# An expert layer whose routing is done ahead of its input rows: logits as products of their own, low parts between the routing steps

## The reference

```python
ys = y * scale
d = rsqrt(einsum('bi,io->bo', ys * ys, weight * weight) + EPS)
y = einsum('bsi,io->bso', x * ys[:, None, :], weight) * d[:, None, :]

lang_probs = softmax(y @ lang_w.T + lang_b)                    # 4 languages
expert_weights = lp_pad[..., idx] + lp_pad[..., idx + 1]       # sums of neighbours
router_probs = softmax(y @ router_w.T + router_b + 0.1 * expert_weights)
top_p, top_i = top_k(router_probs, 2); top_p = top_p / top_p.sum(-1, keepdims=True)
h = gelu(einsum('bsd,edh->bseh', y, w1) + b1, approximate=False)   # 256 -> 1024
expert_out = einsum('bseh,ehd->bsed', h, w2) + b2                  # 1024 -> 256
return x + (top_p[..., None] * take_along_axis(expert_out, top_i)).sum(axis=2)
```

## Time and profile before

| | us |
|---|---|
| median of 3 runs (296.48 to 300.69) | 298.55 |
| the profiled execution | 297.96 |
| its span in the profile | 296.2 |
| TensorE busy | 272.3 |
| ScalarE busy | 195.7 |
| VectorE busy | 189.2 |
| GpSimd busy | 179.4 |
| HBM read and written | 27.61 MB and 9.64 MB |

### The profile page before, as it was taken

How to read it: one execution, slowest core, us unless ns; L and a number is a source line. 1 busy time by engine, 2 the same in 40 slices (tenths; PEclk the granted TensorE clock), 3 DMA queues, 4 the chain that set the end, 5 groups by cost and what they waited for, 6 DMA issues and landing times.

```text
span 296.2 us, 8964 instructions
## 1 busy us (share of the span) xinstructions
PE 272.3 (92%) x3066; PEld 223.1 (75%) x3066; DVE 189.2 (64%) x427; ACT 195.7 (66%) x426; POOL 179.4 (61%) x161
## 2 busy tenths in 40 slices
PE   8999988689999999999999999999999999999800
PEld 6878967588889998777777777777787878778400
DVE  1857788799699788565565565555655656556410
ACT  3356469599697898757767677677676676775500
POOL 8200056884666598676878577777767776464230
PEclk9999999979999999999999999999999999999975
DMA  6899996399874333465574644853544434323130
GB/s 145 325 400 388 353 348 206 109 314 460 306 191 90 56 57 72 56 101 65 76 91 77 87 70 78 76 91 64 83 77 74 75 74 76 51 39 38 20 35 0
DMA packets 39497, 39.93 MB, mean 135 GB/s; under 512 B 19504, under 2 KB 35328, under 8 KB 39296
## 3 DMA queue, kind: packets, MB, share of 16 engines
q1 hardware_dynamic: 31872, 28.89, 32.8%
q0 software_dynamic: 7552, 10.45, 23.0%
q10 hardware_dynamic: 32, 0.01, 0.0%
HBM read 27.61 MB, written 9.64 MB: 126 GB/s over the span
## 4 chain that ended last, share of the span: by engine, by line
PE 82%; DMA 5%; DVE 4%; issue 3%; ACT 2%; POOL 1%; POOLq 0%; DVEq 0%
PE ps L643 33%; PE ps L660 30%; PE ps L539 5%; PE ps L652 4%; PE ps L557 4%; DMA rows<-y_rows,idx 3%; DMA out<-onehot,idx 3%; PE ps L481 1%; PE ps L620 1%; DVE wsp L951 1%; PE ps L512 1%; PE ps L521 1%; ACT wsp L781 1%; PE ps L497 1%; POOL out L470 1%
## 5 line engine op out<-in xcount | busy, mean ns | idle before, releaser
L643 PEld LDWEIGHTS ps<-onehot,wsp 128*128 (+1 forms) x1872 | 130.7, 99 | 34.4 <-issue 1.1
L643 PE MATMUL ps<-onehot,wsp 128*128 128x128 f16 x1872 | 154.2, 220 | 0.8 <-ACT onehot L811 0.6
L827 ACT ACTIVATE pay<-ps,cur 128x128 f32<-128x128 f32 x312 | 117.4, 459 | 51.7 <-issue 37.9
L660 PE MATMUL ps<-wsp,pay 128*128 (+1 forms) x616 | 138.1, 316 | 1.2 <-DVE pay L1113 1.2
L470 POOL DMA_INDIRECT out<-onehot,idx x39 | 67.8, 1739 | 33.7 <-DMA out<-onehot,idx 15.3
L1113 DVE SCALAR_TENSOR_TENSOR pay<-pay,cur 128x512 f16<-128x512 f32 x72 | 54.9, 762 | 29.2 <-ACT pay L815 27.9
L439 POOL DMA_INDIRECT rows<-y_rows,idx x39 | 57.0, 1463 | 17.9 <-issue 11.0
L461 POOL TENSOR_SCALAR onehot<-onehot,cur 128x256 f32<-128x256 f32 x36 | 38.1, 1059 | 24.0 <-DVE onehot L1131 15.8
L660 PEld LDWEIGHTS ps<-wsp,pay 128*128 128x128 f16 x616 | 45.7, 97 | 6.9 <-issue 1.7
L1107 DVE TENSOR_SCALAR pay<-pay,cur 128x512 f16<-128x512 f32 x36 | 18.8, 521 | 26.0 <-ACT pay L827 26.0
L815 ACT ACTIVATE pay<-pay,cur 128x512 f16<-128x512 f32 x36 | 26.0, 722 | 1.2
(11 more groups left out here) (176 smaller groups left out, 195.5 us busy)
## 6 DMA issues: line engine op xcount, KB each, us to landing
stage<-in_L_ffn_w SPq DMA_DIRECT2D x9, 1024.0 KB, 10.6
wsp<-in_L_ffn_w SPq DMA_DIRECT2D x7, 1024.0 KB, 12.0
y_rows<-pay SPq DMA_DIRECT2D x4, 512.0 KB, 9.3
wsp<-in_x SPq DMA_DIRECT2D x3, 512.0 KB, 7.9
b2bc<-in_L_ffn_b SPq DMA_DIRECT2D x1, 1024.0 KB, 4.8
rows<-y_rows,idx POOLq DMA_INDIRECT x39
out<-onehot,idx POOLq DMA_INDIRECT x39, 4.1
wsp<-in_x SPq DMA_DIRECT2D x2, 256.0 KB, 5.5
```

The costliest lines, as they stand in the source:

```text
L643: last = mm(ps[:, HB + (2 * j + g) % RING, c * P:(c + 1) * P], wsp[:, bass.ds(e, 1), o:o + P].rearrange("p a f -> p (a f)"), xsp[:, j % RI ...
L660: last = mm(ps[:, OB + j % 2, 0:width], hsp[:, (2 * j + g) % NH, part, c, :], wsp[:, bass.ds(e, 1), o + w:o + w + width].rearrange("p a f ...
L827: last = a.activation(to, ps[:, HB + (2 * j + g) % RING, c * P:(c + 1) * P], ACT.Gelu, bias=cur[:, j % CURS, cc:cc + 1], scale=cur[:, j % ...
```

## The change

1. **Logits first.** PE makes the logits of all 16 tiles by 32 products of 12 columns (`logits(t)`) between the last transposes, all into one bank; DVE adds the biases in one step of 192 columns. y's rows follow as products of 256 columns in three banks.
2. **Routing beside y's rows.** DVE's low parts of y, now `low_of_y`, stand two by two at eight places between routing steps (`ROWS_AT`). PE does rows 0 to 8 ahead of the counts, 9 to 12 behind them, then the first gram group and rows 13 to 15 among its sums. 19 `keep_warm` products are gone.
3. **Order of the rest.** The probabilities are stored by SP instead of POOL, ahead of y's third store. Gram groups 1, 2 and 3 stand behind the mapping products. POOL's scales of groups 1 and 2 stand among the gathers. ACT splits two halves in place of five ahead of tile 0; halves 4, 6 and 9 stand between copies and gelus.
4. **Experts by eights.** `BATCH` is 8: PE and DVE read `te` four times each (PE the first time ahead of tile 0, then where tiles 16, 24 and 32 begin).
5. **Tail.** ACT weighs tile 36 ahead of the last tile's first gelu instead of behind it.

```diff
-BANKS_Y = 5
+Y_BANKS = (0, 1, 3)
+ROWS_AT = {"in": (0, 1), "best": (2, 3), "second": (4, 5), "picked": (6, 7), "slots": (8, 9), "tiles": (10, 11), "half": (12, 13), "hot": (14, 15)}
-HIGHS = {0: (0, 2, 4, 6, 9), 1: (8, 3), 2: (7,), ...
+HIGHS = {0: (0, 2, 4, 6), 1: (9, 8, 3), 2: (7,), ...
-BATCH = 31
+BATCH = 8
...
             for c in range(4):
-                sp.wait_ge(y_split, 4 * c + 4)
+                sp.wait_ge(y_low, 4 * c + 4)
                 sp.dma_start(y_tiles[:, c // 2, c % 2 * 4:c % 2 * 4 + 4, 0:D],
                              payv[:, 4 * c:4 * c + 4, 0:D]).then_inc(y_written, 16)
...
                 if c == 1:
                     load_weights(9)
+                    sp.wait_ge(p_ready, 1)
+                    for b in range(NB):
+                        sp.dma_start(y_tiles[:, b, :, D:ROW], payv[:, b * TB:(b + 1) * TB, D:ROW]).then_inc(p_written, 16)
             load_weights(3)
             load_weights(7)
...
+            def logits(t):
+                pe.wait_ge(xt_ready, t // 2 + 1)
+                for k in range(KD):
+                    last = mm(ps[:, LB, t * NR:(t + 1) * NR], xT[:, t, k * P:(k + 1) * P], Wyr[:, t // TB, k, D:],
+                              start=(k == 0), stop=(k == KD - 1))
+                return last
             def rows_of_y(t):
-                pe.wait_ge(xt_ready, t // 2 + 1)
-                if t >= BANKS_Y:
-                    pe.wait_ge(lg_read, t - BANKS_Y + 1)
+                if t >= 3:
+                    pe.wait_ge(y_low, t - 2)
...
+            for t in range(9, 13):
+                rows_of_y(t)
+            pe.wait_ge(b1_max, 1)
+            mm(ps[:, SB, BS:BS + E], ...)
+            gram(0)
+            rows_of_y(13)
+            rows_of_y(14)
+            sum_squares(0)
+            rows_of_y(15)
             pe.wait_ge(tok_hot, 1)
...
             last.then_inc(mapped, 1)
+            gram(1)
+            pe.wait_ge(y_low, T)
+            gram(2)
+            sum_squares(1)
             gram(3)
-            keep_warm(WARM, 1, 512)
+            sum_squares(2)
...
             copy_x(0)
+            copy_sums(2)
             copy_x(1)
+            split_high(4)
             gelus(0, 0)
+            split_high(6)
             for j in range(NT):
-                if j == NT - 1:
-                    weigh(NT - 3)
                 gelus(j, 1)
...
+                if j == NT - 2:
+                    weigh(NT - 3)
                 if j + 1 < NT:
                     gelus(j + 1, 0)
...
+            def low_rows(name):
+                for t in ROWS_AT[name]:
+                    dve.wait_ge(y_high, t + 1)
+                    low_of_y(v, t).then_inc(y_low, 1)
...
             pick(0, route, 3, best)
+            scale_of_b1(0)
+            low_rows("best")
...
                 v.tensor_tensor(ohv[:, :, c0:c1], iota[:, :, c0:c1], ...).then_inc(hot_ready, 1)
+                if q == 1:
+                    low_rows("half")
+            low_rows("hot")
```

160 lines of the change are left out of this document (77 added, 83 removed).

## The result

The changed kernel takes **315.7 us**, median of four runs (313.0, 315.0, 316.4, 319.8), where the kernel before has 298.6 (296.5 to 300.7). The ratio is 1.055, interval 1.049 to 1.062. Medians here are of all runs of a kernel; ratios and their intervals leave out runs that were over 1.5% above its fastest. It is slower, as forecast, but by 17 us, not by 6.9, and lies above the range. The profiled execution is the fastest of the four, 313.04 us with a span of 311.3.

What follows compares the result with a forecast made beforehand. PE, busy 92% of the 296.2 us span and nearly unbroken after 60.0 us, passes any shift of the first expert blocks to the end. +6.2 + 1.8 + 0.3 - 1.4 = +6.9 on 297.96 gave 305 us, range 299 to 311.

Steps and rivals of the forecast that it cites:

- second 3 us behind, at 59: Weight halves 3 and 7, issued behind the last low part: first lands at about 56, second at 59; bounds 57 and 65.9.
- hidden behind this: Tile 0's gather lands at 57.8 us, before PE finishes waiting for halves 3 and 7, so it costs nothing.
- PE then waits for ACT, which covers it: 0: A low granted clock around the first expert blocks may come again but costs 0, up to +1.7 us.
- The tail: Tile 36, weighed ahead of the last tile's first gelu, has its scatter bound by the one before: -1.4 us, bounds 0 and -2.4.
- the reads: Expert numbers read by eights, three reads amid full PE blocks: +0.3 us, between 0 and 5.1.
- Logits end 25.3: 32 narrow products at 0.24 us each, with transposes, give the last logit at 25.3 us; routing may begin 8.5 us sooner.
- the clock falls early: Rival: narrow logit products run at the lower clock, 4.8 us later to the end; 310 to 311 us; 0.15 together with full-price reads.
- Last low part 49.9: VectorE's 16 low parts of y, now between routing steps, add 7.65 us; the last ends at 49.9, eating the 8.5 gain.
- T0: Start of tile 0's transposes, behind gram group 3, which waits for halves 3 and 7: 60.6 against 54.4, +6.2 us.
- ACT after T0: ACT's splits of halves 4, 6 and 9 now stand behind T0, making M later: +1.8 us, ends 0 and 5.8.
- M: Start of the block doing tile 2's second half with tile 1's first down half: T0 + 17.4, before 15.6.
- signs that I had named for being wrong: T0 before 57, mapping done before 48, granted clock under 1 before 30 us, or PE gaps at tiles 16, 24, 32.

Runs made afterwards that it cites:

- (10): Changed kernel with nine more 256-column warming products in PE's early gaps, ahead of the logits: 311.9 us, ratio 1.038.
- (3): Changed kernel with y's low parts left out, VectorE writing zeros in their place with all waits kept: 315.9 us.
- (4): Changed kernel with 14 warming products of 512 columns put back on PE ahead of gram group 3: 317.0 us.
- (6): Changed kernel with gram group 3 behind tile 1's first blocks on PE instead of ahead of tile 0's transposes: 316.5 us.
- (7): Changed kernel with halves 3 and 7 and the bias table issued behind tile 0's gather, and gram group 3 behind tile 1's second half: 313.6 us.
- (14): Kernel before with only tile 36 weighed one tile sooner: 296.1 us, ratio 0.9944.
- (2): Changed kernel with ACT's splits of halves 4 and 6 ahead of tile 0's copy instead of between copies and gelus: 312.3 us.
- (13): Kernel before with only its expert numbers read by eights: 297.6 us, ratio 1.0007.
- (12): Changed kernel with late halves 3 and 7, bias table and gram group 3, one read of 31, and nine early warming products: 308.1 us, ratio 1.038.
- (9): Changed kernel with late halves 3 and 7, bias table and gram group 3, ACT's halves 4 and 6 first, and one read of 31: 317.0 us.

## Why the prediction was off, point by point

The way was right, the size was not: the sum lacked 8.2 us of the 15.1 between the profiled spans. Two steps failed. One is the transfer behind the last low part, "second 3 us behind, at 59", with the gather "hidden behind this": from the last low part to the landing of half 7 it took 12.1 us and not 9.1, and the gather landed with it. The other is "PE then waits for ACT, which covers it: 0": the lower clock cost 3.7 us from gram(3) to tile 3. The tail (1.2) and the reads (0.9) were mis-sized.

- **Logits end 25.3; measured 23.8 in the profiled run.** The term of 0.24 us for a narrow product is right on average (32 in 8.1 us), of a faster part and one at the lower level. The transposes took 0.49 us a group and not 0.85: my row for them was itself at the lower level, where one record takes 421 ns for 273 later. In six of the nine profiles with this code a narrow product took 0.43 (1.72 for four) over most of the stretch, and B stands at 28.9 to 31.8. This is the rival "the clock falls early", which I gave 0.15 together with dear reads and priced at 4.8 us. It comes in a part of the runs; it is, by the values of B, the likely difference between the profiled 313.0 and the median of 315.7. With (10) B was early in three profiles of three, without it in three of nine; if the edit did nothing, one draw in eleven would look like this, so it is a sign and no proof. My argument against it was the granted clock under the mapping products. The Trainium skill ("TensorE: Matmul & The Clock Gate", Part 1) has the lower clock as the default; here the level fell while PE did 12-column products and transposes without a gap. That this can happen to a busy PE is what I had not drawn from it.
- **Last low part 49.9; measured 49.0.** From B it is 25.2 us where the sum had 24.6, and the mapping products ran at 47.8 to 50.6 (48.6 to 51.4 in the sum). This step, which eats the gain of the early logits, was right. The low parts are less alone in it than I wrote (3).
- **Halves 3 and 7 land at 59, T0 = 60.6; measured 61.1 and 63.8.** This is the step that failed first. I took 8.6 us for two halves on an emptier queue; they took 11.7 from the first issue, the second by itself 11.1, nearly as before the change. I had the bound (65.9) but sized from a load alone. Of the 3.2 us, 2.1 are this landing and 0.9 are gram(3), which took 1.89 us for 0.95 as PE came out of its wait at the lower level; (4) got that back.
- **"The gather of tile 0 is hidden behind this", landing at 57.8; it landed at 61.3.** The same error seen from the other side: I priced the gather by a row in which no weight half was in flight and put it beside the two halves, which I had just placed there. The bias table's 1 MB was in flight beside that earlier gather too (DMA share 0.75 from 50.6 to 54.0 us); in the changed kernel the share is 1.01 over the gather's 8.6 us. Of the 5.2 us that it took longer, 3.4 are the transfer and 1.8 are POOL's instruction behind VectorE's step, which I had not counted. Each of the two waits hid the other: taking gram(3)'s away gave 1.9 us (6), both together 5.9 us (7).
- **ACT after T0, +1.8, and the clock, 0 (up to 1.7); measured +2.6 to M and +1.65 behind it.** ACT is late at M, as said. But ACT's copy of tile 1 had itself waited for PE's transposes, which stood behind tile 0's 24 products at the lower level (2.72 us for 1.50): 1.2 of the 2.6 are the clock, and 1.4 are left for ACT's order. The 2.6 are measured against a profile with a dip of its own there (15.0 us from tile 0 to M); kernel (14), without one, took 13.4. That is why (2) could take off 3.9: its 13.8 us are nearly all of what ACT's order and the dip had added. My "PE then waits for ACT, which covers it" failed there: the work that slowed was ahead of ACT. (4), with the dip cut to 3.4 us, gained 1.4 between tile 0 and M. The 1.65 is the dip at 82 to 86, behind PE's wait of 3.35 us at M; with ACT's halves first (2) the wait was 0.8 at most and that dip did not come. In the 13 profiles of the changed kernel and its forms the clock fell at M, or in the wait for it, each of the six times that PE waited 3.35 to 3.38 us there, and never in the seven with 0.5 to 2.7. A dip of 3.4 us cost 1.5 to 1.7 us, one of 6.8 us 2.8 to 3.0.
- **Experts by eights, +0.3.** A read of eight took 0.6 to 0.85 us and the last one, of seven, 1.06 to 1.08, so there is no fixed price of 2.8; nor does it go by values alone. But there is no cover between full blocks: three reads cost 2.2 us, and DVE's short first read gives 1.0 back. Net +1.2. In the kernel before it is within 1 us of zero (13): the later reads cost 2.4 there, DVE's shorter one gives 1.05 back, and PE's first, which stands on the path there, 0.7 (from tile 0 to M 12.6 us, against 13.4 in (14)). The 1.6 us that I had estimated from the Trainium skill ("Runtime: NRT & Kernel Launch", Instruction fetch mechanics) was not seen.
- **Tail, -1.4.** Right as a mechanism and as a size, by (14): 0.8 to 2.5 us by its interval. In the changed kernel's profile it gave only 0.2: the scatter of tile 35 left at 285.52 and the next at 292.02, 6.5 us later, held by the landing of the first alone. In eleven of the twelve others with this tail the two are 4.65 to 5.1 us apart, so this profile caught a slow landing; what makes one slow no run shows.

Of the signs that I had named for being wrong, two were there: a granted clock under 1 before 30 us (from 20.8), and gaps on PE at tiles 16, 24 and 32. One number in the rivals doesn't follow from their own terms: the sign turns not from 1.9 of the 7.65 us hidden on, but from 4.3 on a straight line between +6.9 (none hidden) and -5.3 (all).

The sum on the profiled spans: T0 9.4, to M 2.6, the dip behind it 1.65, reads 1.2, rest 0.2: 15.1 us for 6.9 predicted. On top come 2.7 us between the profiled run and the median.

Left open: even the best form (12) is 10 us over the kernel before, 8.1 by the profiles. Of these, 4.0 lie ahead of tile 0: B is 9.1 us sooner and tile 0 13.2 us farther behind it, with y's 16 rows and low parts in between, which no run took apart beyond (3). Another 2.9 lie between tile 0 and M and 2.5 between tiles 3 and 8, where gram(3) and the late halves stand; the tail gives 1.3 back. ACT's order, which (2) showed to cost most of the stretch to M, is untouched in (12); beside (9), no run tried another place for its splits with an early tile 0. What decides in which run the clock falls at 8, at 14 or at 21 us is not known either.

## What to carry to other kernels

Work moved forward is worth only what the last thing behind it gains: here routing started 10 us sooner in the profiled run, but y's low parts filled the time behind it, and then two weight halves, a bias table and the gather were in flight together and arrived together. Price a small indirect transfer by what is in flight at its new time, and where two waits end within a microsecond, count them as one that needs two cures. An engine that idles ahead of the critical step should be given the work that stands behind that step, but only work whose own inputs are there already.
